# Constant matmuls of 448 columns between the steps of a recurrence on one core

## The reference, cut to what matters

```python
def step(carry, inp):
    h, c, n = carry
    xi_t, xf_t, xg_t, xo_t = inp          # x @ W*x + b*, known for all steps
    i_t = jax.nn.sigmoid(xi_t + h @ Wih)
    f_t = jax.nn.sigmoid(xf_t + h @ Wfh)
    g_t = jnp.tanh(xg_t + h @ Wgh)
    o_t = jax.nn.sigmoid(xo_t + h @ Woh)
    c_t = f_t * c + i_t * g_t
    n_t = f_t * n + i_t * jnp.exp(g_t @ Weg + beg)
    h_t = o_t * (c_t / n_t)
    return ((h_t, c_t, n_t), h_t)
```

## Time and profile before

| what | value |
|---|---|
| median of 3 runs | 7952.26 us (7947.48 to 7956.73) |
| span of the profiled execution | 7947.7 us |
| PE busy in the span | 6508.3 us (82%) |
| PEld | 4710.8 us (59%) |
| DVE | 5680.7 us (71%) |
| ACT | 2813.2 us (35%) |
| POOL | 1991.7 us (25%) |
| mean granted clock of PE | 0.795 |

### The profile page before, as it was taken

How to read it: one execution, slowest core, us unless ns; L and a number is a source line. 1 busy time by engine, 2 the same in 40 slices (tenths; PEclk the granted TensorE clock), 3 DMA queues, 4 the chain that set the end, 5 groups by cost and what they waited for, 6 DMA issues and landing times. The chain is left out here.

```text
span 7947.7 us, 238408 instructions
## 1 busy us (share of the span) xinstructions
PE 6508.3 (82%) x89716; PEld 4710.8 (59%) x89716; DVE 5680.7 (71%) x26551; ACT 2813.2 (35%) x7328; POOL 1991.7 (25%) x2075
## 2 busy tenths in 40 slices
PE   8999999999976666666666666679999999999887
PEld 5656656565656565655656565656565655656544
DVE  6676767676767777777777777777666676767566
ACT  4444444444432222222222222234444444444311
POOL 4343535353510000000000000034444353535200
PEclk9999999999975555555555555589999999999898
DMA  0000000000000000000000000000000000000000
GB/s 28 11 4 14 1 14 1 14 1 14 1 15 2 2 2 2 2 2 2 2 2 2 2 2 2 2 4 0 15 11 4 11 4 14 1 14 1 18 2 12
DMA packets 30765, 50.49 MB, mean 6 GB/s; under 512 B 2032, under 2 KB 25291, under 8 KB 28235
## 3 DMA queue, kind: packets, MB, share of 16 engines
q1 hardware_dynamic: 29614, 40.54, 1.6%
q10 hardware_dynamic: 412, 0.42, 0.0%
HBM read 39.91 MB, written 1.05 MB: 5 GB/s over the span
## 5 line engine op out<-in xcount | busy, mean ns | idle before, releaser
L1048 PE MATMUL g_bank<-hbuf,Wgates 128*128 128x2 f32 x2048 | 600.9, 363 | 1024.2 <-DVE hbuf L1136 970.3
L1048 PEld LDWEIGHTS g_bank<-hbuf,Wgates 128*128 128x128 f32 x2048 | 513.0, 311 | 1140.0 <-DVE hbuf L1136 1085.3
L1090 ACT ACTIVATE tg<-g_bank 128x2 f32<-128x2 f32 x1024 | 176.1, 172 | 1690.9 <-PE g_bank L1048 1690.9
L1156 POOL TENSOR_TENSOR xB<-hbuf,xA 128x32 f32 x64 | 16.4, 256 | 2853.0 <-DVE hbuf L1136 2853.0
L371 POOL TENSOR_TENSOR t1b<-t1b,t2b 128x1024 f32<-128x1024 f32 x192 | 451.7, 2354 | 687.1 <-DVE t2b L523 687.1
L371 POOL TENSOR_TENSOR t1a<-t1a,t2a 128x1024 f32<-128x1024 f32 x192 | 451.7, 2354 | 684.7 <-DVE t2a L523 684.7
L1060 PE MATMUL e_bank<-tg,Weg 128*128 128x2 f32 x2048 | 579.4, 352 | 0.0
L1032 PEld LDWEIGHTS s_bank<-hparts,Wparts 128*128 128x128 bf16 x12288 | 571.0, 117 | 0.0
L1110 DVE TENSOR_SCALAR sg<-es 128x4 f32<-128x4 f32 x1024 | 174.4, 170 | 554.5 <-ACT es L1092 554.5
L1060 PEld LDWEIGHTS e_bank<-tg,Weg 128*128 128x128 f32 x2048 | 515.1, 312 | 0.0
L1032 PE MATMUL s_bank<-hparts,Wparts 128*128 128x2 bf16 x12288 | 469.6, 165 | 0.0
(11 more groups left out here) (435 smaller groups left out, 16401.7 us busy)
## 6 DMA issues: line engine op xcount, KB each, us to landing
Wqkv<-in_L_ffn_Wqkv SPq DMA_DIRECT2D x13, 1536.0 KB, 6.5
Wo<-in_L_ffn_Wo SPq DMA_DIRECT2D x13, 512.0 KB, 7.6
W<-in_L_ffn_W SPq DMA_DIRECT2D x12, 341.0 KB
W<-in_L_ffn_W SPq DMA_DIRECT2D x12, 128.0 KB
xt<-in_L_attn_x SPq DMA_DIRECT2D x2, 512.0 KB
rope<-in_rope SPq DMA_DIRECT2D x1, 1024.0 KB, 7.5
out<-ot SPq DMA_DIRECT2D x4, 256.0 KB
W<-in_L_ffn_W SPq DMA_DIRECT2D x12, 42.5 KB
```

The source lines that it names most:

```text
L1048: pe.matmul(g_bank[j][:, s * B:(s + 1) * B], Wg[:, 3, 1, :], h, start=False, stop=True, skip_group_check=True).then_inc(g_done, 1)
L1090: act.activation(tg[:, :], g_bank[j][:, s * B:(s + 1) * B], ACT.Tanh).then_inc(tg_ready, 1)
```

## The change

Behind the product with Weg of each step, and ahead of the step's `project` where it has one, PE gets four (even steps) or three (odd steps) matmuls of the identity with 448 columns of the mask. They write columns 64 to 511 of the same `g_bank`, which nothing reads, wait for nothing and signal nothing. All other instructions stay as they are.

```diff
                 pe.matmul(e_bank[j][:, s * B:(s + 1) * B], Weg[:, :], tg[:, :], start=False, stop=True,
                           skip_group_check=True).then_inc(e_done, 1)
+                for _ in range(3 if s % 2 else 4):
+                    pe.matmul(g_bank[j][:, 64:512], c.identb[:, :], c.mask[:, 0:NT - 1, :].rearrange("p t j -> p (t j)"),
+                              start=False, stop=True, skip_group_check=True)
                 if s % 2 == 1:
```

## The result

| | before | changed |
|---|---|---|
| median of 4 runs | 7949.87 us | 8107.04 us |
| range | 7947.15 to 7956.73 | 8099.57 to 8112.53 |
| span of the profiled execution | 7947.7 us | 8109.4 us |

The ratio is 1.0193, 95% interval 1.0178 to 1.0207: 157 us slower. The forecast was 8138 us, 186 us over the 7952 us that it stood on.

A forecast was written before the change was run, and what follows sets the result against it. The prediction took PE, then ACT and DVE, in series at clock 0.50 as the bound of each recurrence step. Lateness of 2.9 us a chunk over 64 chunks gave 186 us, on 7952 us made 8138 us; range 8040 to 8230.

The forecast's parts named there:

- The clock stays down: In the recurrence, the new matmuls leave PE's clock at 0.50; with a time of 8040 to 8230 us, chance 0.70.
- nearest-row argument: Transpose bursts at 5203 to 5209 us streamed 3.4 of 5.0 us without raising the clock; changed steps stream about 1.3 of 2.9.
- PE is late after a bias projection: In a chunk of 16 steps, four odd bias steps are 0.41 us late each and step s = 0 is 0.78.
- two waits of 0.10 us: Around a bias projection, about 0.10 us is lost at each change between a weight of one row and one of 128.
- 7 x 0.02 + 4 x 0.09 us a chunk: Seven even steps without projection are 0.02 us late each, four odd steps with an input projection 0.09 us each.
- rooms of 1.50 and 1.06 us: Time for new matmuls in even steps without projection (1.50, need 1.52) and odd steps with an input projection (1.06, need 1.15).
- They fit: Rival: PE's idle time before the g gate hides all new matmuls, time within 0.2%, 7952 us; chance 0.03.
- The loads are not hidden: Rival, upper bound: no first weight pass is hidden and each new matmul costs 13 ns more, 8317 us; chance 0.08.
- The clock rival: Rival: in the recurrence the clock rises and stays up, at most 0.18 us gained a step, 7768 us; chance 0.12.

The follow-up runs named there:

- e7: The changed kernel with 24 constant matmuls in the first step of each of the eight rounds in place of four: 8128.77 us, ratio 1.0228.
- e4: The changed kernel with seven constant matmuls in every step in place of four and three: 7852.72 us, ratio 0.9879.
- e6: The changed kernel with six constant matmuls in every step in place of four and three: 8985.85 us, ratio 1.1303.
- e2: The changed kernel with bias projections using a weight of 128 rows, all but row 0 zero, in place of one row: 7981.28 us, ratio 1.0037.
- e1: The changed kernel with only two constant matmuls in s = 0 and in steps with a bias projection: 7957.91 us, ratio 1.001.
- e5: The changed kernel with seven constant matmuls in every step and bias weights of 128 rows: 7790.07 us, ratio 0.9805.

## Why the prediction was right

**The clock stays down.** Shown, by the change's own rows (0.50 from 2400 to 5300 us) and by e7, where it came up and could not be held. The nearest-row argument held: what PE did at 5203 to 5209 us, 3.4 us of columns in 5.0, was more than the change does, 1.3 in 2.9. The row would not have carried much further, though: at 0.373 us a matmul, e4 has 2.61 us of new columns in each of its steps at 1.2 GHz (4.62, 4.62 and about 3.7 us), and its clock came up, while it stayed down with the row's 3.4 us in 5.0. For six or seven matmuls a step the row would have settled nothing; e6 and e4 show how small the step between the two outcomes is. The Trainium skill's rule ("TensorE: Matmul & The Clock Gate", the part on the clock gate), by which activity on the array releases the throttle, agrees with e4 and e7's bursts. The rival that the prediction drew from it, that a PE with hardly any idle time has its clock up, is contradicted by the change and by e6, whose PE records have no gap at 1.2 GHz.

**PE is late after a bias projection.** Forecast 3.13 and 3.50 us for these steps, measured 3.127 and 3.500. Before, a few such steps were longer than the median, so the means give 256 x 0.380 + 64 x 0.735 = 144 us (the prediction's 4 x 0.41 + 0.78 a chunk makes 155), the whole of the stage's 145. That the change of row count is the reason is shown by e2: with 128 rows in all weights the odd steps are not late. In s = 0, where PE stays late and nothing else cuts the gain short, e2 takes 0.43 us off, close to the two waits of 0.10 us and two passes of 0.107 us of its expectation, 0.41.

**The term that was mis-sized** is that of the other steps, 7 x 0.02 + 4 x 0.09 us a chunk, 32 us in all: measured nothing. The step behind it is "the first weight pass of the g gate (0.107 us, 128 columns at 1.2 GHz) is loaded behind the stream and saved", and the same for the input projection: one pass was allowed for, where e6 shows two, 0.21 us. With the second pass the rooms of 1.50 and 1.06 us become 1.61 and 1.17 against 1.52 and 1.15, 0.09 and 0.02 us spare; by e6 they were 0.09 and 0.03.

**Outside the stage** I forecast no change. The medians differ by 157 us, the two profiled executions by 162, and their stages by 145. In those two, 15 us more lie behind the recurrence, half of it in the full attention, where the mean clock over about the same work is lower: 0.85 and 0.81 in the change's stretches of 7853 to 7953 us, 0.93 and 0.90 in 7700 to 7800 before. The code there is the same. Over all ten profiled executions the part behind the last `es` takes from 2752.8 us (e6) to 2775.8 (the change), with 2760.4 before and 2760.2 in e7, which has nearly the change's matmuls. So the 15 us go neither with the added work nor with the delay, and I don't count them to the change; why this part varies stays open.

The number is therefore in part luck: the stage came out 41 us below the 186, and some 15 us from outside it, which no term stood for, brought the total nearer to the forecast.

**The rivals.** "They fit" is right for the work of e1, wrong for the change. "The loads are not hidden" is refuted by the pace (L1056, four in 1.66 us: 3 x 0.373 and a last record of 0.54) and by the steps without projection, which are not late. The clock rival had the right price, 0.18 us a step against 0.171 in e4, but four and three matmuls were too few to bring it about.

## What to carry to other kernels

A constant matmul that fills a wait is free only until the wait ends: take the gap for each kind of step by itself, with what stands between the filler and the next real work, and add only what it holds. In this kernel filling for the clock was all or nothing: at the low clock a filler matmul takes 0.373 us and at the high one 0.188 (seven end after 1.48 us, 0.165 of it behind the last column), so either reach the point where the clock comes up and stays (here seven a step, 1.2% faster, 2% with the bias weights of 128 rows), or leave it out. Six a step cost 13%. Try each count and read the granted clock, since PE's busy share by its records doesn't tell the two cases apart.

A weight of one row between weights of 128 rows is cheap in work and dear in order: padding it with zero rows took 0.40 us off each such place at the low clock, where PE was late, and 0.11 us at the high one (2.665 to 2.554 us, e4 and e5). Where PE waits for h anyway I expect no gain; no run tests that.

## What the runs showed of the hardware

- PE busy for 260.00 of 260 us by its records at a granted clock of 0.50 (e6), and 294.02 of 300 us at 1.00 (e4), with one matmul of 448 columns a step between them.
- At 0.50 a float32 projection and the g gate behind it take 0.40 us more after a stream of 448-column matmuls if the projection's weight has one row instead of 128 (the change and e2).
- Behind such a stream two weight passes of a float32 matmul are loaded under the stream's columns if what they need is there in time: 0.21 us saved (e6).
- At 1.00 the 12 bfloat16 matmuls of `s_bank` take 0.44 us where they wait for nothing and the six of `o_bank` 0.29 us, against 0.46 and 0.30 at 0.50: with 2 columns each they gain next to nothing from the clock. The float32 g gate goes from 0.59 to 0.38 us, the product with Weg from 0.57 to 0.36.
